# Second attention with keys on partitions and summed probability blocks, and a reworked feed-forward

## The reference

```python
att = jax.nn.softmax(jnp.where(mask, -jnp.inf, att), axis=-1)
o = jnp.einsum('bhqk,bkhd->bqhd', att, v).reshape(Bq, CAP, Dq)
x_attn = o @ W_out.T
h2 = rmsnorm(x_sel + x_attn, g2)
x_ff = jax.nn.silu(h2 @ W1.T) * (h2 @ W2.T) @ W3.T
```

```python
q = (x @ Wq.T).reshape(b, t, N_HEADS, HEAD_DIM)
kv_latent = x @ Wkv_down.T
k = (kv_latent @ Wk_up.T).reshape(b, t, N_HEADS, HEAD_DIM)
v = (kv_latent @ Wv_up.T).reshape(b, t, N_HEADS, HEAD_DIM)
scores = jnp.einsum('bqhd,bkhd->bhqk', q, k) * scale
attn = jax.nn.softmax(scores, axis=-1)
out = jnp.einsum('bhqk,bkhd->bqhd', attn, v)
return out.reshape(b, t, N_HEADS * HEAD_DIM) @ Wo.T
```

## Time and profile before

| | |
|---|---|
| median of 3 runs | 2518.78 us (2516.68 to 2521.06) |
| profiled execution, its own time | 2519.22 us |
| its span | 2517.4 us |
| mean granted TensorE clock | 0.938 |
| busy, share of the span | PE 87%, DVE 84%, ACT 72%, POOL 49% |
| second attention (attend_b) | about 1754 to 2320 us |
| first attention (attend_a) | to about 1506 us |

### The profile page before, as it was taken

How to read it: one execution, slowest core, us unless ns; L and a number is a source line. 1 busy time by engine, 2 the same in 40 slices (tenths; PEclk the granted TensorE clock), 3 DMA queues, 4 the chain that set the end, 5 groups by cost and what they waited for, 6 DMA issues and landing times. The chain is left out here.

```text
span 2517.4 us, 62298 instructions
## 1 busy us (share of the span) xinstructions
PE 2198.9 (87%) x22572; PEld 1502.4 (60%) x22572; DVE 2116.7 (84%) x3170; ACT 1817.7 (72%) x2658; POOL 1239.9 (49%) x1482
## 2 busy tenths in 40 slices
PE   5899999999999999999999983556899999999464
PEld 3466667666667666667666663442455555555444
DVE  6899999999999999999999967755899999996674
ACT  1788888888888888888888860115899999996011
POOL 3444444444444444444444443200888888885120
PEclk9999999999999999999999996659899999999766
DMA  2799999999999999999999990006232222221001
GB/s 91 123 192 193 192 186 193 192 192 190 190 192 193 188 192 193 187 193 191 193 190 188 193 172 24 0 8 218 61 72 70 69 71 70 69 69 40 24 1 34
DMA packets 1183690, 333.53 MB, mean 132 GB/s; under 512 B 1145968, under 2 KB 1174512, under 8 KB 1183216
## 3 DMA queue, kind: packets, MB, share of 16 engines
q1 hardware_dynamic: 1182320, 326.97, 73.0%
q10 hardware_dynamic: 1152, 3.62, 0.4%
HBM read 30.57 MB, written 14.68 MB: 18 GB/s over the span
## 5 line engine op out<-in xcount | busy, mean ns | idle before, releaser
L329 PE MATMUL a_out_ps<-a_vs,a_pT 128*128 128x129 f16 x4096 | 726.0, 221 | 48.2 <-ACT a_own_out L378 46.7
L416 DVE SCALAR_TENSOR_TENSOR a_parts<-a_probs,a_parts 128x1024 f16<-128x1024 f32 x512 | 653.2, 1276 | 115.5 <-ACT a_parts L369 115.5
L333 PE MATMUL a_out_ps<-a_vs,a_pT 128*128 128x129 f16 x4096 | 724.4, 219 | 0.0
L331 PE MATMUL a_out_ps<-a_vs,a_pT 128*128 128x128 f16 x4096 | 724.3, 218 | 0.0
L361 ACT ACTIVATE a_probs<-a_score_ps,a_negmax 128x1024 f32<-128x1024 f32 x512 | 572.1, 1117 | 164.9 <-DVE a_negmax L410 164.9
L410 DVE TENSOR_REDUCE a_negmax<-a_score_ps 128x1 f32<-128x1024 f32 x512 | 621.3, 1213 | 2.5 <-PE a_score_ps L315 2.4
L369 ACT ACTIVATE a_parts<-a_probs 128x1024 f16<-128x1024 f32 x512 | 543.4, 1061 | 0.6 <-DMA a_pT<-a_parts 0.6
L329 PEld LDWEIGHTS a_out_ps<-a_vs,a_pT 128*128 128x128 f16 x4096 | 396.5, 97 | 146.1 <-ACT a_own_out L378 99.7
L331 PEld LDWEIGHTS a_out_ps<-a_vs,a_pT 128*128 128x128 f16 x4096 | 403.0, 98 | 44.6
L477 POOL TENSOR_TENSOR acc<-acc,a_own_out 128x256 f32<-128x256 f32 x256 | 248.3, 970 | 351.9 <-DVE a_parts L416 346.5
L311 PE MATMUL a_score_ps<-kh,a_qs 128*128 128x512 f16 x1024 | 388.6, 379 | 10.3 <-DVE a_qs L401 7.0
(11 more groups left out here) (200 smaller groups left out, 2737.0 us busy)
## 6 DMA issues: line engine op xcount, KB each, us to landing
a_pT<-a_parts SPq DMA_TRANSPOSE x512, 4.9
b_qs<-q_parts SPq DMA_DIRECT2D x128, 64.0 KB, 2.0
b_ks<-k_parts SPq DMA_DIRECT2D x128, 64.0 KB, 1.8
q_parts<-b_parts SPq DMA_DIRECT2D x32, 128.0 KB, 1.9
k_parts<-b_parts SPq DMA_DIRECT2D x32, 128.0 KB, 1.9
v_parts<-b_v_all SPq DMA_DIRECT2D x4, 1024.0 KB, 4.6
b_vs<-v_parts SPq DMA_DIRECT2D x32, 128.0 KB, 2.0
b_sent_pT<-b_sent_parts SPq DMA_TRANSPOSE x256, 2.3
```

Source lines behind the costliest of these rows:

```text
L329: pe.matmul(out[:, 0:D + 1], hi, vs[:, G % 2, 0, j, 0:D + 1], start=j == 0, stop=False, skip_group_check=True)
L331: pe.matmul(out[:, 0:D], hi, vs[:, G % 2, 1, j, 0:D], start=False, stop=False, skip_group_check=True)
L333: last = pe.matmul(out[:, 0:D + 1], lo, vs[:, G % 2, 0, j, 0:D + 1], start=False, stop=j == JB - 1, skip_group_check=True)
L416: dve.scalar_tensor_tensor(out=parts[:, T % RING_P, 1, :], in0=probs[:, T % RING_P, :], scalar=PSCALE, in1=parts[:, T % RING_P, 0, :], op0 ...
```

## The change

attend_b is written anew. A unit is still 512 queries of one head. TensorE multiplies twice: first queries on partitions, only to get the row maxima (rate, into the one buffer max_ps; row_max on VectorE), then keys on partitions (scores). The maxima are scaled to fp16 (nm16), spread over the columns by a product with an identity (spread_max), and copied by ScalarE into the 32 further rows of the stacked Q (keep_shift), against which the stacked K holds a constant, so that the second product gives the score less the maximum. ScalarE's exponential then already has keys on partitions, and the product with V follows with no transpose, eight blocks of eight passes in fp32 (times_v). The denominators come from products with ones: GpSimd adds the probability blocks in pairs, and TensorE multiplies the four sums by ones (add_up). VectorE takes the reciprocal of 128 columns and multiplies (keep), both on 128 partitions, since the four column groups hold the 512 queries.

V stays in SBUF in fp32: prepare_b makes no low part of V and doesn't store it. oT has another layout, so project_b multiplies 32 rows at a time, on four row groups, into four banks, with Wo loaded by eight DMAs. In the feed-forward: silu by ScalarE's own function; the division by the softmax's sum moves behind the product with V; half of the masked keys kx are made by ScalarE from a second copy of the product; xh waits for the router scores (junked); and the turns of oh and the copy of the picked rows are ordered anew. The constants and functions of the old attend_b go; they are printed above.

```diff
--- before.py
+++ after.py
...
+        probs = st.sb(s, "b_probs", [P, 2, JB, HALF])
+        sums = st.sb(s, "b_sums", [P, 2, PARTS, HALF])
+        qs = st.sb(s, "b_qs", [P, SLOTS, SEQ], F16)
+        ks = st.sb(s, "b_ks", [P, SLOTS, SEQ], F16)
+        ident16 = st.sb(s, "b_ident16", [P, P], F16)
+        ones = st.sb(s, "b_ones", [P, HDB])
+        negmax = st.sb(s, "b_negmax", [P, 2, TILES])
+        nm16 = st.sb(s, "b_nm16", [P, 2, TILES], F16)
+        inv = st.sb(s, "b_inv", [P, 2, P])
+        max_ps = st.ps(s, "b_max_ps", [P, SEQ])
+        score_ps = st.ps(s, "b_score_ps", [P, 4, HALF])
+        out_ps = [st.ps(s, f"b_out_ps{i}", [P, 2, 2 * P]) for i in range(2)]
...
+            for G in range(heads):
+                slot = G % SLOTS
+                if G >= SLOTS:
+                    sp.wait_ge(scored, 2 * PARTS * (G - SLOTS + 1))
+                for part in range(3):
+                    rows = slice(part * HDB, (part + 1) * HDB)
+                    sp.dma_start(qs[rows, slot, :], q_dram[part // 2, G]).then_inc(qk_in[slot], 16)
+                    sp.dma_start(ks[rows, slot, :], k_dram[part % 2, G]).then_inc(qk_in[slot], 16)
...
+            def rate(u, t):
+                if u >= units:
+                    return
+                slot = u // 2 % SLOTS
+                if t == 0 and u % 2 == 0:
+                    pe.wait_ge(qk_in[slot], 96 * (u // 2 // SLOTS + 1))
+                if u or t:
+                    pe.wait_ge(max_ready, TILES * u + t)
+                cols = slice(u % 2 * HALF + t * P, u % 2 * HALF + (t + 1) * P)
                 for c in range(2):
+                    last = pe.matmul(max_ps[:, c * CH:(c + 1) * CH], qs[0:STACK, slot, cols],
+                                     ks[0:STACK, slot, c * CH:(c + 1) * CH], start=True, stop=True)
+                last.then_inc(rated, 1)
+            def spread_max(u):
+                if u >= units:
+                    return
+                pe.wait_ge(nm_ready, u + 1)
+                if u:
+                    pe.wait_ge(exp_done, PARTS * (u - 1) + 2)
+                for t in range(TILES):
+                    last = pe.matmul(score_ps[:, 3, t * P:(t + 1) * P], nm16[:, u % 2, t:t + 1].broadcast_to([P, P]),
+                                     ident16[:], start=t == 0, stop=True, skip_group_check=True)
+                last.then_inc(spread, 1)
+            def scores(u, pair):
+                if pair == 0:
+                    pe.wait_ge(shift_ready, u + 1)
+                if pair == 3 and u + 1 < units:
+                    pe.wait_ge(shift_ready, u + 2)
+                if u or pair >= 2:
+                    pe.wait_ge(exp_done, PARTS * u + pair - 1)
+                slot = u // 2 % SLOTS
+                for j in (2 * pair, 2 * pair + 1):
+                    last = pe.matmul(score_ps[:, j % 4, :], ks[:, slot, j * P:(j + 1) * P],
+                                     qs[:, slot, u % 2 * HALF:(u % 2 + 1) * HALF], start=True, stop=True)
                 last.then_inc(scored, 1)
+            def times_v(u, pair):
+                if u < 0:
+                    return
+                if pair == 0 and u >= 2:
+                    pe.wait_ge(kept, u - 1)
+                pe.wait_ge(exp_done, PARTS * u + pair + 1)
+                out = out_ps[u % 2]
+                for j in (2 * pair, 2 * pair + 1):
+                    for t in range(TILES):
+                        last = pe.matmul(out[t * HDB:(t + 1) * HDB, 0, 0:P], v_all[:, u // 2, j, :],
+                                         probs[:, u % 2, j, t * P:(t + 1) * P], start=j == 0, stop=j == JB - 1,
                                          skip_group_check=True)
                 last.then_inc(pv_done, 1)
+            def add_up(u):
+                if u < 0:
+                    return
+                for pair in range(PARTS):
+                    pe.wait_ge(added, PARTS * u + pair + 1)
+                    for t in range(TILES):
+                        last = pe.matmul(out_ps[u % 2][t * HDB:(t + 1) * HDB, 0, P:], ones[:],
+                                         sums[:, u % 2, pair, t * P:(t + 1) * P], start=False,
+                                         stop=pair == PARTS - 1, skip_group_check=True)
+                last.then_inc(den_done, 1)
+            pe.wait_ge(consts, 3)
+            for t in range(TILES):
+                rate(0, t)
+            spread_max(0)
+            for t in range(TILES - 1):
+                rate(1, t)
+            for u in range(units):
+                scores(u, 0)
+                scores(u, 1)
+                rate(u + 1, 3)
+                times_v(u - 1, 2)
+                times_v(u - 1, 3)
+                add_up(u - 1)
+                spread_max(u + 1)
+                rate(u + 2, 0)
+                scores(u, 2)
+                scores(u, 3)
+                rate(u + 2, 1)
+                times_v(u, 0)
+                times_v(u, 1)
+                rate(u + 2, 2)
+            times_v(units - 1, 2)
+            times_v(units - 1, 3)
+            add_up(units - 1)
...
+            def exponentiate(u, pair):
+                act.wait_ge(scored, PARTS * u + pair + 1)
+                if u >= 2:
+                    act.wait_ge(pv_done, PARTS * (u - 2) + pair + 1)
+                    act.wait_ge(added, PARTS * (u - 2) + pair + 1)
+                at = 2 * pair % 4
+                act.activation(probs[:, u % 2, 2 * pair:2 * pair + 2, :], score_ps[:, at:at + 2, :],
+                               ACT.Exp).then_inc(exp_done, 1)
+            def keep_shift(u):
+                if u >= units:
+                    return
+                act.wait_ge(spread, u + 1)
+                act.copy(qs[STACK:P, u // 2 % SLOTS, u % 2 * HALF:(u % 2 + 1) * HALF],
+                         score_ps[STACK:P, 3, :]).then_inc(shift_ready, 1)
+            keep_shift(0)
+            for u in range(units):
+                exponentiate(u, 0)
+                exponentiate(u, 1)
+                keep_shift(u + 1)
+                exponentiate(u, 2)
+                exponentiate(u, 3)
...
+            def row_max(u, t):
+                if u >= units:
+                    return
+                dve.wait_ge(rated, TILES * u + t + 1)
+                dve.tensor_reduce(negmax[:, u % 2, t:t + 1], max_ps[:], AX.X, ALU.max,
                                   negate=True).then_inc(max_ready, 1)
+                if t == TILES - 1:
+                    dve.wait_ge(max_ready, TILES * (u + 1))
+                    dve.tensor_scalar(nm16[:, u % 2, :], negmax[:, u % 2, :], 1.0 / SHIFT, None,
+                                      ALU.mult).then_inc(nm_ready, 1)
+            def keep(u):
+                if u < 0:
+                    return
+                dve.wait_ge(den_done, u + 1)
+                dve.reciprocal(inv[:, u % 2, :], out_ps[u % 2][:, 0, P:]).then_inc(inv_ready, 1)
+                dve.wait_ge(inv_ready, u + 1)
+                dve.tensor_tensor(oT[:, u, :], out_ps[u % 2][:, 0, 0:P], inv[:, u % 2, :], ALU.mult).then_inc(kept, 1)
+            dve.memset(ks[STACK:P, :, :], SHIFT / HDB).then_inc(consts, 1)
+            for t in range(TILES):
                 row_max(0, t)
+            for t in range(TILES - 1):
+                row_max(1, t)
+            for u in range(units):
+                row_max(u + 1, 3)
+                row_max(u + 2, 0)
+                keep(u - 1)
+                row_max(u + 2, 1)
+                row_max(u + 2, 2)
+            keep(units - 1)
...
+            pool.tensor_scalar(ident16[:], ident[:], 1.0, 1.0, ALU.mult, ALU.mult).then_inc(consts, 1)
+            pool.memset(ones[:], 1.0).then_inc(consts, 1)
+            for u in range(units):
+                for pair in range(PARTS):
+                    pool.wait_ge(exp_done, PARTS * u + pair + 1)
+                    if u >= 2:
+                        pool.wait_ge(den_done, u - 1)
+                    pool.tensor_tensor(sums[:, u % 2, pair, :], probs[:, u % 2, 2 * pair, :],
+                                       probs[:, u % 2, 2 * pair + 1, :], ALU.add).then_inc(added, 1)
...
+                if c == NCH - 4:
+                    act.wait_ge(sel_done, 2)
+                    act.copy(xsel[:], sel[:])
                 act.wait_ge(ohT_done, c + 1)
                 act.copy(ohT[:, 4 * c:4 * c + 4, :], tps[:]).then_inc(ohT_kept, 1)
-            act.wait_ge(sel_done, 2)
-            act.copy(xsel[:], sel[:])
 
...
             pool.wait_ge(ln.normed, NT)
+            pool.wait_ge(junked, NT)
             pool.tensor_tensor(xh[:], x[:], xn[:], ALU.add)
...
                     pick(b - 1)
+                if 1 <= b < NB - 1:
                     turn(b - 1)
             pick(NB - 1)
+            turn(NB - 2)
             turn(NB - 1)
...
                 chained(dve.reciprocal(rd[:, pr], dn[:, pr]))
-                dve.tensor_tensor(pr_[:, pr], pr_[:, pr], rd[:, pr, :, None].broadcast_to([P, HA, CAP]),
-                                  ALU.mult).then_inc(probs_ready, 1)
```

(56 more changed lines are left out.)

378 lines of the change are left out of this document (43 added, 335 removed).

## The result

The changed kernel takes 2509.86 us (median of 7 runs, 2509.36 to 2512.11), the kernel before 2519.63 (median of 7 beside them). The ratio is 0.9964, with a 95% interval of 0.9952 to 0.9976: 0.36% faster, where 2527 was forecast, 0.3% slower. The span of the profiled execution is 2508.1, its granted clock 0.947.

A forecast was written before the change was run, and what follows sets the result against it. The prediction took the second attention to be bound by waits around the one max_ps, with the scaling held by GpSimd's sum. Its terms: 2519.2 + 60 (second attention) - 2.8 (prepare_b) - 11.1 (project_b) - 38 (feed-forwards) = 2527 us, range 2466 to 2552.

The forecast's parts named there:

- 62 periods of 9.5: Second attention's main loop: 62 units of 512 queries at 9.5 us each, 589 us of the stage's 626.5.
- the ring of one buffer: Second attention: each product into max_ps waits for the maximum before it; once round 8.67 us, 9.5 with the scaling held.
- R2: Third of a unit's four products into max_ps in the second attention; the next unit's was forecast 9.47 us later.
- R0: First of a unit's four products into max_ps, forecast 5.24 us behind R2 with the scaling held.
- 0.17 and 0.05: Second attention: the scaling's duration after GpSimd's sum and the delay until it is seen, 0.22 us together.
- The unheld period: Second attention: time per unit if the scaling need not wait for GpSimd's sum, 8.67 us.
- R3 to R0: Second attention: from a unit's fourth product into max_ps to the next unit's first, 2.53 us by TensorE's order, unheld.
- the faster rival: Second attention: the scaling is not held by GpSimd's sum, period 8.67, kernel 2477 us; chance 0.24.
- The feed-forward: Savings from silu, later normalising, xh's wait and new turns: 19.0 us in each of two, 38 in all.
- TensorE as a whole: Rival for the second attention: TensorE binds, blocks cost 0.36 also in a row, period 9.85, kernel 2548 us; chance 0.06.
- the clock: Rival: TensorE's clock does not hold in the second attention, period near 12.9, kernel 2737 us, in part 2600; chance 0.06.
- the four row groups of project_b: project_b: forecast to run together, saving 14.3 us before added loads; the rival, in turn, gave 2570 us, chance 0.03.

The follow-up runs named there:

- e1: The changed kernel with the scaling of the four maxima moved from VectorE to ScalarE: 2483.96 us.
- e2: The changed kernel with GpSimd's second pair sum of each unit waiting for the scaling of the next unit's maxima: 2483.61 us.
- e9: The changed kernel with a column of zeros as the exponential's bias, output unchanged: 2517.45 us.
- e7: The changed kernel with the exponential also writing row sums that nobody reads: 2516.77 us.
- e11: The changed kernel with the scaling of the maxima run over 512 columns instead of 4, the rest zeros: 2527.49 us.
- e10: The changed kernel with GpSimd's sum xh no longer waiting for the router scores: 2529.44 us.
- e5: The changed kernel with the scaling on ScalarE (e1), plus the two banks of max_ps used as two half buffers: 2421.96 us.
- e3: The changed kernel without GpSimd's pair sums, the products with ones running over all eight probability blocks: 2540.15 us.
- e6: The changed kernel with the scaling on ScalarE (e1), plus the products with ones moved behind the next unit's first product into max_ps: 2475.79 us.

## Why the prediction was wrong in its sign

The forecast was a small difference of large terms, and the size of one of them was off. The step that failed is the term "62 periods of 9.5". The period is 9.24; 62 x 0.26 = 16 of the 17.1 us. Its mechanism stands, by e1 and e2: the ring of one buffer binds, and the scaling in it is held by GpSimd's sum. Counted from R2, link by link:

| from R2 | forecast | measured | |
|---|---|---|---|
| first exponential ends | 2.20 | 2.10 | no bias column: 1.02 for 1.12 (e9) |
| GpSimd's second sum ends | 4.80 | 4.69 | the same 0.10 |
| R0 | 5.24 | 5.00 | 0.11 from above, 0.13 from the scaling |
| next R2 | 9.47, taken as 9.5 | 9.24 | R0 to R2 is 4.23 and 4.24 |

- **The exponential**, 0.10. The sum took the row of before for an instruction that has neither a bias column nor a row sum any more. Without the bias column it is 0.09 shorter (e9); the row sum would have put its signal 0.09 later (e7), and from its end to GpSimd's start the estimate of 0.1 stands against 0.08.
- **The scaling**, 0.13. It was held, as chosen, but "0.17 and 0.05" behind the hold was wrong: it ends 0.02 behind the sum, since the first 0.15 of it run under the hold (e11). The forecast's own row said so: in the earlier trace rows the held operation, taken to be worth 0.28, ends at 1554.06, only 0.14 behind the sum's 1553.92.
- **What is held.** The reciprocals of the earlier trace rows, which stood against a hold, did run beside GpSimd: by the trace 200 of the 256 start while an instruction of GpSimd is running, and none takes more than 0.164. In the changed kernel 126 maxima out of PSUM and 62 products with an input in PSUM start beside a running sum and keep their 1.23 and 0.29. So whether an operation waits goes by its form, and the scaling is of a form that does (e2).
- **Rounding** 9.47 to 9.5, 0.03.
- **The unheld period** was forecast as 8.67 and is 8.82 (e1, e2). R3 to R0 is 2.65 for 2.53: the eight blocks cost 0.217 each, as forecast, and the changes to column groups and back 0.09 and 0.15 (0.53 less 0.44, and 1.89 less 8 x 0.217), where 0.15 was taken for both. While the scaling is held this is hidden. It makes the faster rival 2484 where 2477 stood.
- **The other stages.** Ahead of the first product attend_b takes 4.2 us for 4.3. The fill and the tail together are within 1 us of the sum. prepare_b is right. Of project_b the four row groups run together, as said; the seven loads more cost 1.9 instead of 3.2, and the first chunks gain less than the later ones.
- **The feed-forward** gave 40.6 for 38. The parts of the sum are there: from the gate's exponential to the products with W3 8.44 were read before, 1.85 after, so 6.6; the second transposes start 8.52 behind the first masked score for 12.80, so 4.3; e10 shows xh. Two small things were not in it. The masked keys, taken at 0 with a bound of +1, bring 1.3 in each, less 0.2 by which they start later, with one product more ahead of them. And the products with W3 take 1.99 for 2.93: their granted clock was 0.77 in this kernel's window and 0.50 in the one of before, behind a pause of TensorE of 1.9 us and of 8.5.
- **The rivals.** TensorE as a whole does not bind (e5: the same products in a shorter period), the clock stayed at 1.00, and the four row groups of project_b don't work in turn. What TensorE has between R3 and R0 does count once the hold is gone (e3, e6).

What settles the sign is then 0.26 us in a ring that runs 62 times; the chance for slower, 0.53, was that of a forecast only 8 us above the kernel before, against a known error of 0.15 on the period that is worth 9.

Left open: the silu, the place of the normalising and the masked keys were not undone one by one; their shares are read from the timelines.

## What to carry to other kernels

A loop around one buffer runs at the sum of its links, whatever the engines' totals say; splitting that buffer in two halves was worth 62 us here. Price an instruction in the form that it will have (with or without bias column, with or without accumulator), since a tenth of a microsecond on the ring is worth 6 us in 62 periods. When two engines must not meet, move the small operation to a third engine or let the long one wait for it: both gave 26 us for an edit of a few lines.
